# Two attention and FFN layers on one core: one register per expert work item, and seven moved steps

## What is computed

```python
# layer 0, attention (per batch)
scores = einsum('bdhn,bdhm->bhnm', rope(Wq @ x + bq), rope(Wk @ ctx + bk)) / sqrt(HD)
x = x + Wm @ (softmax(scores) @ (Wv @ ctx + bv)) + bm
# layer 0, experts: relu2(t) = relu(t) ** 2
topk_weights = normalised sigmoid scores of the 2 chosen experts
h1 = einsum('th,ehi->tei', x, w_up)
a = relu2(h1) * combine[:, :, None]
routed = einsum('tei,eih->th', a, w_down)
shared = relu2(x @ shared_up) @ shared_down
# layer 1, attention: softmax(rmsnorm(q) @ rmsnorm(k).T * scale) @ v, 32 heads
# layer 1, FFN: x @ W.T + bias + delta of the 2 chosen low-rank experts
```

## Time and profile before

| | us |
|---|---|
| median of 3 runs | 391.71 (391.51 to 392.6) |
| profiled execution, own time | 395.81 |
| its span, first to last instruction | 393.7 |
| mean granted TensorE clock | 0.879 of full |
| PE, DVE busy | 295.4 (75%), 274.0 (70%) |
| ACT, POOL busy | 172.8 (44%), 100.3 (25%) |
| DMA, mean over the span | 135 GB/s |

### The profile page before, as it was taken

How to read it: one execution, slowest core, us unless ns; L and a number is a source line. 1 busy time by engine, 2 the same in 40 slices (tenths; PEclk the granted TensorE clock), 3 DMA queues, 4 the chain that set the end, 5 groups by cost and what they waited for, 6 DMA issues and landing times.

```text
span 393.7 us, 7219 instructions
## 1 busy us (share of the span) xinstructions
PE 295.4 (75%) x2620; PEld 184.1 (47%) x2620; DVE 274.0 (70%) x708; ACT 172.8 (44%) x288; POOL 100.3 (25%) x200
## 2 busy tenths in 40 slices
PE   4256888888777678899996989315588884969877
PEld 3113444444434333786676868203354552543535
DVE  6967889989988865488805643135488887687881
ACT  1103367476575565255335676002477665430101
POOL 1135246346342220205731111174300100000000
PEclk9855899999999986689998999855599999888997
DMA  7593456857853022001243666783637655100001
GB/s 246 153 268 100 135 157 217 275 134 228 263 142 109 21 77 97 2 0 53 95 136 118 229 227 215 235 232 93 179 112 208 171 167 163 40 1 0 28 27 53
DMA packets 70306, 53.20 MB, mean 135 GB/s; under 512 B 4864, under 2 KB 67072, under 8 KB 70272
## 3 DMA queue, kind: packets, MB, share of 16 engines
q1 hardware_dynamic: 64640, 41.76, 35.4%
q10 hardware_dynamic: 4096, 6.79, 5.4%
q0 software_dynamic: 1536, 4.20, 3.3%
HBM read 30.90 MB, written 21.63 MB: 133 GB/s over the span
## 4 chain that ended last, share of the span: by engine, by line
PE 43%; DVE 33%; issue 7%; DMA 6%; ACT 5%; POOL 4%; SPq 2%; DVEq 0%; POOLq 0%; ACTq 0%
DVE mx L1571 9%; PE psum L715 4%; PE psum L818 4%; PE psum L832 4%; PE psum L1020 3%; PE psum L664 3%; PE psum L1032 3%; DVE pvT L1920 2%; PE psum L877 2%; DVE rope_ab L1560 2%; PE psum L1122 2%; PE psum L996 2%; PE psum L679 2%; PE psum L805 2%; PE psum L700 2%
## 5 line engine op out<-in xcount | busy, mean ns | idle before, releaser
L1571 DVE TENSOR_REDUCE mx<-psum 128x2 f32<-128x512 f32 x128 | 81.0, 683 | 14.5 <-PE psum L679 13.5
L1163 ACT ACTIVATE prob<-psum 128x1024 f32<-128x1024 f32 x64 | 64.0, 1022 | 43.1 <-PE psum L700 43.1
L679 PE MATMUL psum<-kstk,qstk 64*128 64x256 bf16 x256 | 27.1, 293 | 21.8 <-DVE mx L1571 12.1
L715 PE MATMUL psum<-prob,vt 128*32 128x256 f32 x512 | 37.0, 402 | 4.8 <-ACT prob L1163 3.7
L1343 ACT ACTIVATE prob<-psum 128x1024 f32<-128x1024 f32 x32 | 31.9, 1019 | 13.0 <-PE psum L980 13.0
L475 POOL TENSOR_TENSOR parts<-qk_rest,parts 128x256 bf16<-128x256 f32 (+1 forms) x15 | 13.5, 900 | 55.7 <-ACT parts L1317 52.2
L700 PE MATMUL psum<-qstk,kstk 64*128 64x256 bf16 x256 | 26.2, 292 | 0.8 <-DMA qstk<-mT 0.8
L679 PEld LDWEIGHTS psum<-kstk,qstk 64*128 64x128 bf16 x256 | 9.8, 97 | 35.0 <-DVE mx L1571 23.8
L996 PE MATMUL psum<-prob,vt 128*32 128x128 f32 x512 | 21.7, 292 | 4.5 <-ACT prob L1343 4.5
L805 PE MATMUL psum<-eye,xn 128*128 128x128 f32 x32 | 7.7, 329 | 22.3 <-DVE xn L1855 14.9
L715 PEld LDWEIGHTS psum<-prob,vt 128*32 128x32 f32 x512 | 16.5, 113 | 14.0 <-ACT prob L1163 5.4
(11 more groups left out here) (252 smaller groups left out, 621.8 us busy)
## 6 DMA issues: line engine op xcount, KB each, us to landing
qstk<-stack_scratch SPq DMA_DIRECT2D x32, 256.0 KB, 3.5
stack_scratch<-parts SPq DMA_DIRECT2D x23, 192.0 KB, 2.1
kstk<-key_scratch SPq DMA_DIRECT2D x16, 256.0 KB, 4.3
kstk<-stack_scratch SPq DMA_DIRECT2D x14, 256.0 KB, 6.0
stack_scratch<-parts SPq DMA_DIRECT2D x25, 128.0 KB, 2.1
wup<-in_wup ACTq DMA_DIRECT2D x4, 640.0 KB, 4.6
wdn<-in_wdn ACTq DMA_DIRECT2D x4, 640.0 KB, 6.0
prob<-sorted_x SPq DMA_DIRECT2D x8, 256.0 KB, 4.1
```

The costliest lines, as they stand in the source:

```text
L679: last = nc.tensor.matmul(banks[s][:, nb * D:(nb + 1) * D], qstk[par][rows, pair, nb * P:(nb + 1) * P], kstk[par][rows, pair, :], start=Tr ...
L715: last = nc.tensor.matmul(pv_bank(1)[32 * j:32 * j + 32, g * D:(g + 1) * D], vt[b % 2][:, mb, 4 * t + j, 8:40] if low else vt[b % 2][:, mb ...
L1163: nc.scalar.activation(prob[(b * PAIRS + k) % 3][:], exp_buf(k).rearrange("p a n -> p (a n)"), ACT.Exp, scale=SCALE).then_inc(exp_done, 1)
L1571: nc.vector.tensor_reduce(mx[:, half, :, 4 * s + p4:4 * s + p4 + 1], bank.rearrange("n (b m) -> n b m", b=2), AX_X, ALU.max).then_inc(misc ...
```

## The change

1. **One register.** `xt_all`, `wup` and two small buffers become parts of one tensor `low`. The turned tiles are placed in reverse, so that the address of tile t − e is TILES−1−t plus e, and the register with the expert gives both addresses. PE loads 16 and 15 values in the shared FFN, and nothing in the expert loop; DVE's chain for the owner loses two instructions.
2. **DVE at the experts.** The first copies of turned tiles stand ahead of `rest_keys(0)`, and `expert_weights` stands behind the loop.
3. **SP.** The last key parts stand behind store 12 instead of 13; the key stacks of batches 0 and 1 wait for the gathers of these batches, and batch 2's stand behind the queries of batch 1.
4. **Router.** `rank` stands ahead of `project_keys(3)`.
5. **First attention.** Max transposes at spots 7 and 15 instead of 6 and 14, so behind `pv`; DVE's evacuation of `v+wm` moves from spot 9 to 10, behind the next pair of maxima, and PE's use three banks later waits for one evacuation more (`late`).
6. **Layer 1's prologue.** On DVE, step `qT` of batch 0 moves ahead of the normalisation of batch 2.

```diff
-        wup = sb("wup", [P, 2, NCH, INTER])
...
-        xt_all = sb("xt_all", [P, SORTED, 2, P])
-        xnT = xt_all[:, 0:NB].rearrange("p t f n -> p (t f n)").rearrange("p (f n) -> p f n", f=2)
+        low = sb("low", [P, SORTED - 1 + SORTED + NCH, 2 * P])
+        wup = low[:, SORTED - 1 + SORTED:].rearrange("p s n -> p (s n)").rearrange("p (f e i) -> p f e i", f=2, e=NCH)
+        low_flat = low[:, 0:SORTED - 1].rearrange("p s n -> p (s n)")
+        xnT = low_flat[:, 0:2 * TOK].rearrange("p (f n) -> p f n", f=2)
...
-        owner = sb("owner", [1, 2, TILES])
+        owner = sb("owner", [1, TILES])
         inv_var = sb("inv_var", [P, NB])
-        owner_i = sb("owner_i", [1, 2, TILES], I32)
+        owner_i = sb("owner_i", [1, TILES], I32)
...
-        rel = [sb(f"rel{i}", [P, HALF]) for i in range(2)]
-        act2 = [sb(f"act2{i}", [P, HALF]) for i in range(2)]
+        rel = [low_flat[:, 2 * TOK + i * HALF:2 * TOK + (i + 1) * HALF] for i in range(2)]
+        act2 = [low_flat[:, 2 * TOK + 2 * HALF:2 * TOK + 3 * HALF], sb("act21", [P, HALF])]
...
-            return xt_all[:, 2 * n:2 * n + 2].rearrange("p t f n -> p (t f n)")
+            return low[:, 2 * (SORTED - 1) - 2 * n - 1:2 * (SORTED - 1) - 2 * n + 1].rearrange("p t n -> p (t n)")
...
-        MAXT = {0: {2: (0, 1), 8: (1, 0), 14: (1, 1)}, 7: {}}
-        MAXT.update({b: {6: (b + 1, 0), 14: (b + 1, 1)} for b in range(1, 7)})
+        MAXT = {0: {2: (0, 1), 8: (1, 0), 15: (1, 1)}, 7: {}}
+        MAXT.update({b: {7: (b + 1, 0), 15: (b + 1, 1)} for b in range(1, 7)})
...
-                if n in (2, 6, 10, 13):
-                    p = (2, 6, 10, 13).index(n)
+                if n in (2, 6, 10, 12):
+                    p = (2, 6, 10, 12).index(n)
...
-            for b in range(SETS):
+            for b in range(2):
+                sp.wait_ge(gathered[b], 32)
                 keys_c_from_dram(b)
             for b in range(NB):
-                if b >= SETS:
+                if b >= 2:
                     keys_c_from_dram(b)
...
-                pe.wait_ge(misc_free, u - 3 + banks_of(use))
+                late = any(u == A_AT["v+wm", x] + 3 for x in range(NB - 1))
+                pe.wait_ge(misc_free, u - 3 + banks_of(use) + late)
...
             project_keys(2)
+            rank()
             project_keys(3)
-            rank()
             up(0, 0)
             up(0, 1)
-            experts, rows = [], []
-
-            def load_counted(first, last):
-                experts.extend(counted(0, mybir.EngineType.PE, first, last))
-                rows.extend(counted(1, mybir.EngineType.PE, first, last))
-
+            experts = []
             for n in range(2 * N_SHARED):
                 down(n // N_SHARED, n % N_SHARED)
                 if n + 2 < 2 * N_SHARED:
                     up((n + 2) // N_SHARED, (n + 2) % N_SHARED)
-                if n in (2, 3, 4):
+                if n in (3, 4):
                     pe.wait_ge(owner_ready, 1)
-                    load_counted(8 * (n - 2), 8 * (n - 1))
+                    experts.extend(counted(mybir.EngineType.PE, 16 * (n - 3), min(16 * (n - 2), TILES)))
...
+                        last = nc.tensor.transpose(psum[:, 6 + n % 2, (2 - 2 * t_ + f) * P:(3 - 2 * t_ + f) * P],
                                                    tile_x(n)[:, (2 * t_ + f) * P:(2 * t_ + f + 1) * P], eye[:])
...
+                                                low[:, TILES - 1 - tile:TILES - 1 - tile + NE, f * P:(f + 1) * P][:, bass.ds(experts[tile], 1), :
+                                                                                            ].rearrange("p o n -> p (o n)"),
                                                 start=(f == 0), stop=(f == 1))
...
                 if 0 <= n + 1 < TILE_PAIRS:
-                    tile_up(n + 1, rows)
+                    tile_up(n + 1, experts)
                 if n >= 0:
                     tile_down(n, experts)
-                if 6 <= n < 10:
-                    load_counted(2 * n + 12, min(2 * n + 14, TILES))
                 if n in (4, 7):
...
                         flip_back(b - 1)
                     for use in a_uses(b, spot):
+                        if use[0] != "v+wm" or b == NB - 1:
+                            a_use(use, misc(A_AT[use]), A_AT[use])
+                    if spot == 10 and b + 1 < NB:
+                        use = ("v+wm", b)
                         a_use(use, misc(A_AT[use]), A_AT[use])
...
-            steps.then(nc.vector.tensor_copy(begin_i[:, 0, 0:NE - 1], begin[0:1, 1:NE]))
+            steps.then(nc.vector.tensor_scalar(begin_i[:, 0, 0:NE - 1], begin[0:1, 1:NE], float(SORTED * P - 1), None,
+                                               ALU.min))
...
-            steps.then(nc.vector.tensor_reduce(owner[:, 0, :].unsqueeze(2), lot, AX_X, ALU.add))
-            nc.vector.tensor_copy(owner_i[:, 0, :], owner[:, 0, :])
-            steps.then(nc.vector.tensor_tensor(owner[:, 1, :], work_no[:, :, 0], owner[:, 0, :], ALU.subtract))
-            nc.vector.tensor_scalar(owner_i[:, 1, :], owner[:, 1, :], float(NE), float(SORTED - 1), ALU.add, ALU.min
-                                    ).then_inc(owner_ready, 1)
+            steps.then(nc.vector.tensor_reduce(owner[:].unsqueeze(2), lot, AX_X, ALU.add))
+            nc.vector.tensor_copy(owner_i[:], owner[:]).then_inc(owner_ready, 1)
 
             number = rows[:, 3 * NE:4 * NE].unsqueeze(1).broadcast_to((P, NB, NE))
...
             dve.wait_ge(y_free, 2)
-            expert_weights()
-            rest_keys(0)
             for n in range(TILE_PAIRS + 2):
                 if n < ROW_PAIRS:
                     take_turned(n)
                 if n >= 2:
                     take_tile_y(n - 2)
-                if n in (4, 8, 11):
-                    rest_keys(n // 4 + n // 11)
+                if n in (1, 4, 8, 11):
+                    rest_keys((1, 4, 8, 11).index(n))
+            expert_weights()
             attend_norm(0, 1)
             center(0, 0)
             c_pro(("v", 0))
...
             center(1, 1)
             c_pro(("q", 0))
             c_pro(("xT", 1))
+            c_pro(("qT", 0))
             attend_norm(2, 1)
```

13 lines of the change are left out of this document (5 added, 8 removed).

## The result

The changed kernel takes 381.01 us (median of 4 runs, 380.21 to 382.48) beside 392.15 us of the kernel before (the median of four, three of which are those of the 391.71): a ratio of 0.9721, 95% interval 0.9684 to 0.9758. That is 11.1 us less; 11.5 less were forecast, 380.2 us.

The account below looks back on a forecast made before the run. No engine bounds the whole span: DVE, nearly PE, in the first attention, PE in shared FFN and experts, DMA waits from 248 to 262. Eight terms sum to −11.5 us, 391.71 to 380.2; 8-in-10 range 375.5 to 386.

Parts of the forecast that it names:

- T1: Start of the experts: DVE's first copy of turned tiles, and PE's tile_up(0) behind it, come 2.0 us earlier.
- T2: Start of the experts: with PE's idle stretch shortened, the clock holds in the next four microseconds, −1.5 us.
- T3: Expert loop: without PE's register loads tile_up(10) no longer waits behind the pair after tile_down(9), −1.7 us.
- T4: SP's queue: the last key parts move ahead of store 13, so the last store is issued earlier, −1.2 us.
- T5: First gather: without key-stack loads beside it, it lands in 2.9 us instead of 6.24, −3.3 us.
- T6: Layer 1's prologue: DVE's subtraction for qT(0) ahead of a normalisation shortens PE's wait, −1.1 us.
- T7: Router: rank one projection earlier makes PE stall for hot while the experts gain nothing, +0.3 us.
- T8: First attention: max transposes behind pv and add_output later; middle batches 0 ± 0.15 each, batch 6 −0.8, in all −1.0 us.
- Rival (a): Last batch of the first attention: the clock holds there too, 3.5 us more gain, 376.7 us; 18%.
- Rival (d): Wait at 250 to 262 is bound by bytes: T4 and T5 give −0.5 each, T3 nothing; 385.9 us, 5%.
- the likeliest case: Whole kernel: the forecast itself, 380.2 us, given 50% with its own range of 378 to 382.5 us.
- signs that the prediction named for being wrong: First-attention batches over 0.3 us off 15.2, an unchanged wait for gathers, or a later stage (264 on) longer than now.

Follow-up runs that it names:

- keys_alone: Kernel before, with only the key-stack loads of batches 0 and 1 made to wait for those batches' gathers; 0.9925 of before.
- after: The changed kernel with all parts of the change, as first timed and profiled; 381.01 us, 0.9721 of before.
- after_again: The changed kernel with no edit, timed a second time beside the other runs; 0.9724 of before.
- maxt_back: Changed kernel with the max transposes ahead of pv again (spots 6 and 14), v+wm's evacuation still one spot later; 0.9768 of before.
- vwm_back: Changed kernel with v+wm's evacuation at spot 9 and PE's wait as before, max transposes still behind pv; 0.9646 of before, 378.86 us.
- same_again: The kernel before with no edit, profiled and timed a second time; 0.999 of before, profiled execution 392.34 us.
- loads_back: Changed kernel with PE's fourteen register loads put back, six in the shared FFN and eight in the expert loop; 0.9727 of before.
- vwm_rank_back: Changed kernel with v+wm's evacuation at spot 9, PE's wait as before, and rank behind project_keys(3) again; 0.9694 of before.

## Why the forecast held, step by step

- **T1, first copy**: −1.8 measured, −2.0 forecast. The copy starts 0.77 us behind the turn's start (203.16 to 203.93), not 0.57.
- **T2, clock at the experts' start**: −1.64 measured, −1.5 forecast. With the old order it fell in three of four profiles (5.86 us; keys_alone had 4.21 with the same wait of 2.28 us), with the new one in none of ten. A mean gain is so about 1.2. The forecast took the fall as one that every execution has. (The page of before has an 8 in its clock row at this place, not a 5 or 6; what shows the fall is the window's 0.57.)
- **T3, register loads**: −1.5 measured, −1.7 forecast, at the place named, `tile_up(10)`; the loads stood behind `tile_down(8)`, not 9, and `tile_down(9)` comes only behind it. The two loads of 16 and 15 values took 1.30 and 1.86 us, and no cost of theirs shows in the stretch.
- **T4, SP's order**: −1.0 measured, −1.2 forecast.
- **T5, first gather**: −3.1 measured, −3.3 forecast, shown by keys_alone.
- **T6, qT(0)**: −1.1 both, and not given back.
- **T7, rank**: forecast +0.3, measured +0.75 where the router's clock is down for 6.8 us (47.38, the mean of four, against 46.63, the mean of three) and nothing where it is down for 10.2 (48.28 against 48.37). PE's wait for `hot` was to be 0.13 us and is 0.47 in after: PE is free 0.32 us before DVE's instruction ends (170.94, 171.26), and starts 0.15 behind it, which was left out. The projection, cut in two, takes 1.89 and 1.97 us where it took 3.62 in one row. These two make 0.7. In after_again, with its clock down for longer, PE comes to `rank` only when `hot` is there, and doesn't wait. Over the seven kernels with rank ahead that is +0.4.
- **T8, first attention**: in batches 1 to 4 the forecast set 0.65 us of lateness from the moved add against 0.5 to 0.6 from `pv` ahead of the transposes, and took 0 ± 0.15. maxt_back and vwm_back show the two halves for themselves, +0.2 and −0.6 against before, and together they give +0.04, more than their sum. Batch 6 gives −0.6 (−0.8 forecast). The late DMA in batches 1 and 2, 0 to 1.2 us in the seven kernels that keep the whole of the change's attention part, was not foreseen at all. By structure T8 is −0.6 to +0.6.
- **Rival (a)**, the clock in the last batch, was given 18% for a further 3.5 us. Its mechanism is true of a part of the executions: with the transposes ahead of `pv` the clock fell in the last batch or the end of batch 6 in three of five profiles (13.4 us, and maxt_back's batch 6), with them behind in none of nine. That is 2.9 us in about every second execution. That the kernel before loses them in each, as its one profile suggests, is wrong (same_again).
- **Rival (d)** was priced half a microsecond too high: with T4 and T5 at −0.5 each and T3 at nothing its sum is −6.3, so 385.4 us and not 385.9. keys_alone and loads_back rule it out in any case.

The measured terms: −1.8 −1.2 −1.5 −1.0 −3.1 −1.1 (T1 to T6); −0.6 for the router's stretch (48.37, the mean of four, to 47.77, the mean of seven: +0.4 of rank and −1.0 of the clock, down for 6.8 us instead of 10.2 in four of the seven); −0.2 for T8 by structure (−0.64, and 0.4 of late DMA in the mean of seven); −1.5 for the clock of the last batch (half of 2.9). That is −12.0, where −11.1 was measured with an interval of −9.5 to −12.4. Left out of this sum is what lies behind qT(0): 119.8 to 121.4 us in the five kernels built on before, 118.6 to 122.8 in the nine built on after, 0.9 more in the mean. It moves with the clock there (granted 0.91 in after_again's 118.6, 0.86 in after's 121.7), and since the two executions of after alone lie 3.1 us apart, these 0.9 can't be put down to the change.

So the forecast's time was right by its six terms at the experts and behind them, which gave −9.7 of −10.8, and in the rest by errors that cancel, which is luck: the last batch's clock and the router's, which the likeliest case left out, gave what the late DMA, the mean of T2 and perhaps the stage behind qT(0) took. The profile's own difference, −14.3, is 3 us too large mostly because before's execution was one in which the clock fell in the last batch.

Of the signs that the prediction named for being wrong, the wait for gathers did not keep its length (12.93 us to 6.71). The two others did appear in the profile after: a batch of the first attention of 15.57 us, 0.37 off 15.2, which is the late DMA, and a stage from qT(0) to the end of 121.7 us instead of 121.0, which is within what executions of one kernel differ by.

Open: what decides whether the router's clock is down for 6.8 or for 10.2 us. It was 10.2 in all four kernels with the attention as before, in three of the nine with the transposes behind `pv`, and not in maxt_back; that the attention's part makes the shorter one likelier isn't shown, as no run held the clock. Nor is it shown by a run that ACT's load makes the 12 KB late. That vwm_back beats after is likely (0.9646 against 0.9721 and 0.9724), but vwm_rank_back, which should have been better still, was not: its profile has 3.3 us of late DMA and 122.4 us behind qT(0), against 0.95 and 119.5. The 0.6 us of each batch are sure, what of them is left behind the late DMA is not.

## What to carry to other kernels

Take the length of each stretch, not the time of the whole, to test a term: from the first result copy to qT(0) the stretches that an edit doesn't touch repeat within 0.1 us in the changed kernel and within 0.5 in the one before, where executions differ by several microseconds. Look at the clock first, though: the router's stretch and the stage behind qT(0) differ by 1.1 and 3.1 us between two executions of one program. Two moves made together can cancel (transposes behind `pv`, and the evacuation one spot later), and only running each alone shows it. Large loads that nobody needs for 20 us cost 3.1 us here, as they were issued beside the small transfer that everybody waits for: have them wait for it.
